# Up projection recomputed from PSUM and two gated products over magnitudes in a quantised feed-forward block

## What is computed

```
def act_qdq(x):                       # 16 bits, one scale for the whole tensor
    scale = jnp.maximum(jnp.max(jnp.abs(x)) / 32767.0, 1e-12)
    return jnp.clip(jnp.round(x / scale), -32768.0, 32767.0) * scale
x    = act_qdq(layernorm(x))
up   = act_qdq(x @ lpbq_dequant(w_up).T)       # 128 -> 384 columns
gate = act_qdq(x @ lpbq_dequant(w_gate).T)
sig  = fixed_qdq_u16(jax.nn.sigmoid(gate))     # 16 bits, fixed scale
gate = act_qdq(gate * sig)
o    = act_qdq(gate * up)
out  = o @ lpbq_dequant(w_down).T
```

## Time and profile before

| | |
|---|---|
| median of 3 runs | 343.34 us (343.32 to 343.42) |
| span of the profiled execution | 341.2 us |
| PE busy | 279.0 us (82%) |
| DVE busy | 252.5 us (74%) |
| ACT busy | 192.6 us (56%) |
| GpSimd busy | 136.7 us (40%) |

### The profile page before, as it was taken

How to read it: one execution, slowest core, us unless ns; L and a number is a source line. 1 busy time by engine, 2 the same in 40 slices (tenths; PEclk the granted TensorE clock), 3 DMA queues, 4 the chain that set the end, 5 groups by cost and what they waited for, 6 DMA issues and landing times. The chain is left out here.

```text
span 341.2 us, 4468 instructions
## 1 busy us (share of the span) xinstructions
PE 279.0 (82%) x1424; PEld 160.7 (47%) x1424; DVE 252.5 (74%) x538; ACT 192.6 (56%) x303; POOL 136.7 (40%) x274
## 2 busy tenths in 40 slices
PE   0889899899989779985007888899998998999994
PEld 0558544455434345331005776664654654444462
DVE  5699875877996388889989977986596693441834
ACT  1673367556476746779589632446656446665232
POOL 6669893750050411870002059921386207131100
PEclk9999999999999999997556999999999999999998
DMA  7930100010000000000000002220001000000004
GB/s 204 336 146 3 69 32 10 27 73 10 1 8 3 0 0 2 1 0 0 1 0 0 2 0 92 94 100 2 10 25 76 8 0 10 1 0 3 0 1 123
DMA packets 9687, 12.55 MB, mean 37 GB/s; under 512 B 896, under 2 KB 5376, under 8 KB 9664
## 3 DMA queue, kind: packets, MB, share of 16 engines
q1 hardware_dynamic: 9232, 11.80, 9.7%
q10 hardware_dynamic: 432, 0.47, 0.7%
HBM read 4.27 MB, written 1.05 MB: 16 GB/s over the span
## 5 line engine op out<-in xcount | busy, mean ns | idle before, releaser
L1333 DVE TENSOR_REDUCE sb_nm<-ps_top 128x3 f32<-128x462 f32 (+2 forms) x168 | 96.0, 626 | 26.6 <-PE ps_top L953 13.9
L772 ACT ACTIVATE sb_pr<-ps_score 128x512 f32<-128x512 f32 (+1 forms) x148 | 82.3, 583 | 58.8 <-PE ps_score L985 49.2
L953 PE MATMUL ps_top<-sb_Kd,sb_Q 128*128 128x462 f32 (+3 forms) x240 | 69.7, 349 | 4.7 <-DVE sb_nm L1333 2.4
L985 PE MATMUL ps_score<-sb_Q,sb_Kd 128*128 128x512 f32 x119 | 54.4, 467 | 1.3 <-ACT sb_pr L772 1.0
L953 PEld LDWEIGHTS ps_top<-sb_Kd,sb_Q 128*128 128x128 f32 x240 | 42.6, 188 | 18.1 <-DVE sb_nm L1333 11.9
L626 POOL TENSOR_SCALAR sb_var<-sb_mv 128x4 f32<-128x4 f32 x16 | 4.7, 291 | 83.3 <-DVE sb_mv L1296 82.9
L985 PEld LDWEIGHTS ps_score<-sb_Q,sb_Kd 128*128 128x128 f32 x119 | 22.2, 188 | 31.6 <-ACT sb_pr L772 23.4
L1017 PE MATMUL ps_pv<-sb_pr,sb_V 128*32 128x512 f32 x256 | 34.1, 605 | 0.0
L620 POOL TENSOR_SCALAR_AFFINE_SELECT sb_pr<-sb_pr 128x512 f32<-128x512 f32 x16 | 10.6, 661 | 46.4 <-ACT sb_pr L772 46.4
L1353 DVE STREAM_TRANSPOSE sb_oq<-ps_pv 128x512 f32<-128x512 f32 x16 | 10.8, 700 | 12.4 <-PE ps_pv L1017 12.3
L643 POOL TENSOR_SCALAR sb_xn<-sb_xr,sb_nmean,sb_rstd 128x128 f32<-128x128 f32 x44 | 19.3, 453 | 1.2
(11 more groups left out here) (180 smaller groups left out, 556.5 us busy)
## 6 DMA issues: line engine op xcount, KB each, us to landing
sb_Q<-sb_qh SPq DMA_DIRECT2D x16, 256.0 KB, 2.3
sb_Q<-sb_ql SPq DMA_DIRECT2D x8, 256.0 KB, 3.3
sb_xr<-x SPq DMA_DIRECT2D x4, 256.0 KB, 7.7
out<-sb_xr SPq DMA_DIRECT2D x4, 256.0 KB, 2.5
sb_wsb<-w SPq DMA_DIRECT2D x1, 704.0 KB, 9.0
sb_wf<-wffn SPq DMA_DIRECT2D x1, 576.0 KB, 8.6
sb_wkr<-wkr SPq DMA_DIRECT2D x2, 256.0 KB, 7.1
sb_Q<-sb_nmT SPq DMA_DIRECT2D x16, 32.0 KB
```

The source lines that it names most:

```text
L772: act.activation(pr[:, k % PRING, q0:T], score_bank(B * layer + b, t)[:, q0:T], ACT.Exp, scale=SCALE).then_inc(exp_r, 1)
L953: ins = pe.matmul(cols[:, c0:c1, :], Q4[n % 3][:, g, P * qt:P * qt + P], Kd[n % 3][:, g, j:j + c1 - c0, 0:keys], start=True, stop=not mask ...
L985: ins = pe.matmul(ps[:, :], Kd[n % 3][:, g, j, 0:P], Q4[n % 3][:, g, :], start=True, stop=True, skip_group_check=True)
L1333: dve.tensor_reduce(nm[:, :, :].rearrange("p t h -> p (t h)")[:, f0:f0 + heads], top[k % MRING][:, 0:keys * heads].rearrange("p (h k) -> p ...
```

## The change

Twelve up tiles are multiplied three times instead of once. Tiles 12 to 23 serve only DVE's maximum, which now reads PSUM. Tiles 24 to 35 are read from PSUM by ACT for the magnitudes, tiles 36 to 47 for the signed 16-bit form. No fp32 copy of up is kept. Gate tiles are reduced by DVE in PSUM first and copied by ACT afterwards. gate16 of batch 1 moves to ACT. For batches 2 and 3 (BY_SIZE) the gated product is taken over magnitudes, in one instruction with its maximum; the sign of the gate is multiplied onto the signed up (`signs`, `signed_up`), and last16 uses these. Batch 0's last16 and last product go in thirds, all on ACT; batch 2's last16 goes in thirds too. down(3) moves behind maximum unit 2 of layer 1 and ffn_residual(3) behind unit 6. q_low moves ahead of statistics 1, and GpSimd's clears move.

On PE:

```diff
+        def up_bank(t):
+            return fbank[t % FRING] if t < 43 else (fbank[1], fbank[2], fbank[3], fbank[6], fbank[0])[t - 43]
...
             def down(c):
-                pe.wait_ge(*((xo_r, c) if c > 0 else (xod_r, 1)))
-                for t in range(TT):
-                    for m in range(NF):
+                for m in range(NF):
+                    if c == 0 or m == 0:
+                        pe.wait_ge(xo_r, m + 1 if c == 0 else NF + c)
+                    for t in range(TT):
...
                             scores_for_top(layer, b, u)
+                            if (layer, i, b, u) == (1, -1, 0, 2):
+                                down(B - 1)
...
+                    def bank_read(t):
+                        if t < 12:
+                            pe.wait_ge(fev, t + 1)
+                        elif t < 24:
+                            pe.wait_ge(fam_r, t + 1)
+                        elif t < 36:
+                            pe.wait_ge(uabs_r, t - 23)
+                        else:
+                            pe.wait_ge(u16_r, t - 35)
...
                         if t >= FRING:
-                            pe.wait_ge(fev, t - FRING + 1)
-                        pe.matmul(fbank[t % FRING][:, :], wfT[:, 3 * (t // 12) + m, :], xq[:, c, :],
+                            bank_read(t - FRING if t < 46 else t - 5)
+                        pe.matmul(up_bank(t)[:, :], wfT[:, 3 * (t >= 12) + m, :], xq[:, c, :],
                                   start=True, stop=True).then_inc(fmm, 1)
...
-                    for k in range(2, 4):
-                        global_top(k)
-                    pe.wait_ge(fev, 24)
-                    pe.wait_ge(o_r, 2)
-                    keep_warm(6)
+                    for t in range(13):
+                        linear(t)
+                    global_top(1)
+                    for t in range(13, 31):
+                        linear(t)
+                    global_top(2)
+                    for t in range(31, 36):
+                        linear(t)
+                    global_top(3)
+                    for t in range(36, 45):
+                        linear(t)
                     global_top(4)
-                    keep_warm(2)
+                    for t in range(45, 48):
+                        linear(t)
                     pe.wait_ge(sc_r, 5)
-                    keep_warm(4)
-                    for c in range(3):
+                    pe.wait_ge(u16_r, 5)
+                    keep_warm(2, score[1])
+                    for c in range(2):
                         down(c)
                     turn_normed("pre", 1, 0)
                     project_q(1, 0)
-                    down(3)
+                    down(2)
                     turn_normed("pre", 1, 1)
+                    pe.wait_ge(u16_r, 12)
```

On ACT, the new queue behind the copies of the gate tiles (`up(c)` is three pieces of 512, each waiting for its tile):

```diff
+                    gate16(1)
                     for c in range(B):
-                        up_size(c)
-                    for c in range(B):
-                        product_size(c)
-                    up16(0)
-                    up16(1)
-                    product16(2)
-                    up16(2)
-                    product16(3)
-                    up16(3)
-                    product(1)
-                    product(2)
-                    product(3)
+                        if c in BY_SIZE:
+                            gate_size(c)
+                        sigmoid16(c)
+                    for t in range(24, 36):
+                        up_size(t)
+                    product_size(0)
+                    product_size(1)
+                    product_size(3)
+                    up(0)
+                    product16(1)
+                    up(1)
+                    for m in range(NF):
+                        product(0, slice(m, m + 1), m + 1)
+                    up(2)
+                    product(1, slice(0, NF), NF + 1)
+                    up(3)
+                    product(2, slice(0, NF), 2 * NF + 1)
                     copy_normed("pre", 1, 0)
                     copy_q(1, 0)
+                    product(3, slice(0, NF), 2 * NF + 2)
```

On DVE, the new instructions and the queue behind the last gate tile (as it stands after the change):

```diff
+                def gated_size(c):
+                    dve.wait_ge(s16_r, c + 1)
+                    dve.wait_ge(gabs_r, c - 1)
+                    dve.tensor_tensor_reduce(out=flat(gf, c), in0=flat(gabs, c - BY_SIZE[0]), in1=flat(s16, c), scale=1.0,
+                                             scalar=0.0, op0=ALU.mult, op1=ALU.max,
+                                             accum_out=amax[:, 3, c:c + 1]).then_inc(am_r, 1)
+
+                def signs(c):
+                    dve.wait_ge(g16_r, c)
+                    dve.tensor_scalar(flat(sign, c - BY_SIZE[0]), flat(g16, c), -1.0, 1.0, ALU.max, ALU.min).then_inc(sign_r, 1)
+
+                def signed_up(c):
+                    dve.wait_ge(sign_r, c - 1)
+                    dve.wait_ge(u16_r, NF * c + NF)
+                    sg = flat(sign, c - BY_SIZE[0])
+                    dve.tensor_tensor(sg, up16(c).rearrange("p m t -> p (m t)"), sg, ALU.mult).then_inc(us_r, 1)
```

On GpSimd:

```diff
             def clear_early():
-                pool.wait_ge(fmm, 24)
-                pool.wait_ge(o_r, B)
+                pool.wait_ge(fmm, 4 * 12)
+                pool.wait_ge(n3_r, NF)
                 pool.memset(Q4[1][:, :, :].bitcast(F32), 0.0).then_inc(q4_clear, 1)
+                pool.memset(Q4[2][:, :, :].bitcast(F32), 0.0).then_inc(q4_clear, 1)
```

More of the change, by code:

```diff
@@ L1184, in _, with linear @@
                     keep_warm(3, top[1])
-                    for t in range(24):
+                    def bank_read(t):
[7 more added lines that the diff above has]
+                            pe.wait_ge(u16_r, t - 35)
+                    def linear(t):
                         c, m = t % 12 // 3, t % 3
@@ L1470, in outer @@
[L1470 to L1476 removed]
+                    dve.wait_ge(uabs_r, NF * c + NF)
@@ new lines, in outer, with last16 @@
+                    dve.wait_ge(*((n2d_r, 1) if c == 2 else (n2abs_r, min(c, 2) + 1)))
+                    dve.tensor_tensor_reduce(out=flat(uabs, c), in0=n2abs(c).rearrange("p m t -> p (m t)"), in1=flat(uabs, c),
+                                             scale=1.0, scalar=0.0, op0=ALU.mult, op1=ALU.max,
+                                             accum_out=amax[:, 4, c:c + 1]).then_inc(o_r, 1)
+                def last16(c, m=slice(0, NF)):
+                    part = lambda t: t[:, m, :].rearrange("p m t -> p (m t)")
+                    if c in BY_SIZE:
+                        dve.wait_ge(us_r, c - 1)
+                        left, right = n2abs(c), sign[:, c - BY_SIZE[0], :, :]
+                    else:
+                        dve.wait_ge(*((n2_r, 1) if c == 0 else (n2a_r, 1)))
+                        dve.wait_ge(u16_r, NF * c + m.stop)
+                        left, right = g16[:, c, :, :], u16[:, c, :, :]
+                    dve.scalar_tensor_tensor(out=part(uabs[:, c, :, :]), in0=part(left), scalar=sc[:, 4, 3:4], in1=part(right),
@@ L1512, in ffn @@
-                for t in range(14, 24):
+                for t in range(19, 24):
                     absmax(t)
                 part_max(2, 12)
-                gated(2)
+                gated_max(1)
                 whole_top(2)
                 scale_of(2)
-                gated_max(2)
-                gated(3)
-                gated_max(3)
+                for c in BY_SIZE:
+                    gated_size(c)
                 part_max(3, B)
+                signs(2)
                 whole_top(3)
@@ L1523, in ffn @@
                 scale_of(3)
-                product16(0)
-                factor(1, 1.0, sc[:, 3, 1:2], sc[:, 2, 1:2])
-                for c in range(B):
-                    outer(c)
-                part_max(4, B)
-                product16(1)
+                product_size(2)
+                factor(1, 1.0, sc[:, 3, 1:2], sc[:, 2, 1:2])
+                outer(2)
+                outer(0)
+                outer(1)
+                outer(3)
+                part_max(4, B)
+                product16(0)
@@ L1530, in ffn @@
                 whole_top(4)
                 scale_of(4)
-                last16(0)
-                dve.wait_ge(n3_r, 1)
-                dve.tensor_scalar(flat(gf, 0), flat(n2abs, 0), sc[:, 4, 1:2], None, ALU.mult).then_inc(xod_r, 1)
+                for m in range(NF):
+                    last16(0, slice(m, m + 1))
                 last16(1)
-                last16(2)
+                signed_up(2)
                 ffn_residual(0)
                 norm_stats("pre", 1, 0)
-                last16(3)
+                for m in range(NF):
+                    last16(2, slice(m, m + 1))
@@ L1540, in ffn @@
+                signs(3)
                 norm("pre", 1, 0)
                 ffn_residual(1)
+                signed_up(3)
+                last16(3)
+                q_low(1, 0)
                 norm_stats("pre", 1, 1)
                 ffn_residual(2)
-                q_low(1, 0)
-                norm("pre", 1, 1)
-                ffn_residual(3)
```

(3 more changed lines are left out.)

123 lines of the change are left out of this document (61 added, 62 removed).

## The result

The changed kernel takes 347.17 us, median of 4 runs (345.93 to 347.55); the kernel before takes 343.37 beside it (343.32 to 343.42). The ratio is 1.0104, 95% interval 1.0086 to 1.0122: slower by 3.8 us. The profiled execution is the fastest of the four, 345.93 with a span of 344.0, against 341.2 before.

A forecast was written before the change was run, and what follows sets the result against it. No engine alone bounds the quantised block, but a chain of global maxima through DVE and PE. With +0.4 at layer 1's start and +3.5 in its ramp, 343.34 + 3.9 = 347.2 us, range 342.2 to 349.8.

The forecast's parts named there:

- Scale 1: Start of the quantised block: DVE reduces gate tiles in PSUM without ACT's copy first; ready at 145.85, gain 0.55.
- Scale 2: Quantised block, batch 2's turn of DVE's queue and PE's spreading: 165.6, gain 2.8, or 4.3 if the clock holds.
- Scales 3 and 4: Later quantised block: scale 3 at 172.2, gain 3.5; scale 4 at 182.4, gain 5.5.
- Half given back before the norm: Scale 4 to batch 0's norm: down(0) waits behind tile 47 until 189.1; norm at 196.4, gain 2.8.
- signed_up: DVE's product of sign and up around batch 0's norm: 1.8 us each, only signed_up(3) on the path.
- The query path: Behind batch 0's norm: takes 3.35 as before; q_low starts at 201.6, ends at 202.35, gain 2.1.
- Layer 1 released by GpSimd: Border to layer 1: PE starts 5.5 behind q_low's end, after batch 1's norm and transpose, at 207.85, 0.4 later.
- down(3) in the ramp: Layer 1's first maximum units: 2.8 for the matmuls plus 0.7 for the residual, 3.5 us added.
- (1): PE's clock holds in every gap: layer 1 starts at 204.75, the ramp adds 3.5, 344.1 us; chance 0.17.
- (2): Scales' gain reaches layer 1, down(3) fits between units: layer 1 at 202 to 203, 338.6 to 341.7 us; chance 0.16.
- (3): Colder: layer 1's first units with down(3) run at 1.2 GHz, 1.7 more, 348.9 us; chance 0.12.
- (4): GpSimd's clearing holds DVE, or GpSimd's root comes late, 1.6 more, 348.8 us; chance 0.05.

The follow-up runs named there:

- after: The changed kernel itself, with nothing further edited; 347.17 us.
- a1_down3_back: Changed kernel with down(3) back ahead of batch 1's transpose and ffn_residual(3) back behind statistics 2; 344.16 us.
- c1: b4 with the gated product over magnitudes and its maximum as two instructions instead of one; 337.88 us.
- b4: a4 plus dummy matmuls ahead of tile 26 and of batch 0's transpose; 336.14 us.
- a3: Changed kernel with up(2) ahead of the thirds of product(0) on ScalarE; 342.52 us.
- b1: Changed kernel with dummy matmuls in four PE gaps, no work moved, one PE wait now ahead of batch 1's transpose; 342.95 us.
- a2: Changed kernel with batch 1's statistics back ahead of q_low on DVE; 344.14 us.
- b3: Kernel before the change with q_low put ahead of statistics 1 on DVE; 346.70 us.
- a4: Changed kernel with the edits of a1_down3_back, a2 and a3 together; 339.39 us.
- b2: Kernel before the change with down(3) put behind maximum unit 2 and ffn_residual(3) behind unit 6; 348.32 us.

## Why the prediction came out right, and where it did not

The forecast of 347.2 stands beside 347.17, but the profiled execution is 345.93, and a closeness of 0.03 is luck: errors that cancel, and a clock that differs from execution to execution. What was right is the mechanism, step by step:

- **Scale 1**, 145.85 by the sum: ready at 145.67, with a gate16 taken up at 145.71. Right.
- **Scale 2**, 165.6 with a fall of the clock, 164.1 without: 163.88 in after's profile, which held, and 165.55 in that of a1_down3_back, where it fell. Both branches were sized to 0.3; which is taken changes from execution to execution, and the sum could name only one.
- **Scales 3 and 4**: 16.8 from scale 2 to scale 4 by the sum, 16.80 in the profile. The fused products, signs under the spreading, the end of the 2.65 beside GpSimd's clearing, all as told; c1 prices the fusing at 1.4 to 1.9, in b4.
- **Half given back before the norm**: tile 47 at 3.2 behind scale 4 by the sum, 3.5 measured; down(0) at 6.7 against 7.0; the norm at 14.0 against 14.5. The mechanism is the one named, and a3 shows it by taking it away: 4.7 us at down(0). One reading in it is wrong: DVE's 2.45 us (last16(2) in thirds and signs) were said to cover GpSimd's root, whose rows come to 1.67 + 1.03 = 2.7 and some 0.1 of handing over. In after the root's last row ends at 195.11, signs at 195.07, and the norm starts at 195.21, 0.10 behind the root as in the kernel before. So the root still releases the norm, at a cost of about 0.2 us.
- **signed_up**, mis-sized: 1.8 taken, 0.96 measured. The nearest row was of another operation. signs took 0.55 where 0.5 was taken. The Trainium skill ("VectorE: DVE Perf Modes", the perf-mode tier table) has tensor_tensor at two elements a cycle where all is 16-bit, and the prediction's estimate from it was 0.9; the trace agrees.
- **The query path**, missed: q projection at half clock, 2.00 where 1.10 stands in b1, so that the path took 4.24 where 3.35 was taken. DVE waited 0.87 for it, which took up the 0.84 that signed_up had saved. q_low came 5.36 behind the norm, 5.2 by the sum.
- **Layer 1 released by GpSimd**: transpose and unit 0 5.2 behind the end of q_low against 5.5. Right in kind; a2 and b3 show it both ways.
- **down(3) in the ramp**, 3.5 by the sum: 2.95 in after, which is DVE's 2.21 of idle time and the residual's 0.74. The 2.8 for the matmuls were partly covered by units 0 to 2. a1 takes it away.
- **Layer 1's first score**, missed: 0.74 later still, with a wait of 0.90 for the DMA of the turned maxima, where there was none before. Why that DMA lands later is open.

So the shifts are -0.96, +2.95 and +0.74, together 2.7 of the 2.8 between the spans, where the sum had +0.4 and +3.5. With the clock lost at tile 26, 1.7 more, it would be 4.4. The median of four, 3.8 above before, lies between. In the case that the forecast assumed, with the fall, the shifts would thus be 4.4 and not 3.9.

**The rivals.** (1) The clock holds everywhere, 344.1: b1 made it so and gave 342.95; 1.2 less than the rival's time, since unit 0 came at 204.10 where 204.75 was forecast, and the ramp cost 2.9 where 3.5 was. (2) The gain reaches layer 1, 338.6 to 341.7: not in the change. a4, where down(0) follows the rounding by 2.3 us, gave 339.39, in the rival's range; but its down(3) was taken out of the ramp and does not fit between the units as the rival had it, and layer 1 started at 203.96, not before 203.3. (3) Colder: not in after's profile, but in a3, b2 and b3, at 1.6 to 1.8 (17.95 and 17.93 against 16.38, 15.27 against 13.43), near the 1.7 of the prediction. (4) GpSimd's clearing: its two clears end at 189.91, before the root for batch 0 is asked for at 192.74; the root itself cost about 0.2, as said above, and not 1.6.

## What to carry to other kernels

Here a chain made 7 us shorter brought nothing, since the queues behind it were in the wrong order for the new pace. After such a cut, follow each in-order queue to the next border and ask, for every step moved, what gap it filled before and who stands behind its new wait. A matmul that fills a gap can pay twice, in its own time hidden and in the clock that the next matmuls have (b2: 4.5 us in the ramp for 2.84 us of matmuls and a residual of 0.74). Where PE waits between short bursts on a path of dependences, try a few dummy matmuls in each gap before anything else, and look at the spread of the runs as well as at their median.

## What the runs showed of the hardware that was not expected

- The same gap of 2.45 us ahead of the same tile left PE at 2.4 GHz in two profiled executions and at 1.2 GHz in three. One more or less of these is 1.5 to 1.7 us, half a per cent of the kernel. The versions with four gaps of 2.5 us and more, or most of them, repeat less well: a1, a2 and a3 spread over 3.6 to 3.7 us in ten runs each, b1 with dummies in the gaps over 1.4 in eleven.
- VectorE on 1536 elements a partition, all int16: 0.55 us for an operation with a constant (signs), 0.96 for a product of two tensors (signed_up), but 1.75 to 1.82 for the product of two tensors with rounding or with a maximum (last16, outer). A plain product of two int16 tensors written as fp32 took 1.76 in c1. So both the form of the instruction and the type of every tensor in it decide.
- GpSimd beside VectorE: in the timeline of GpSimd in after, the root's two instructions for batch 0 stand beside VectorE's thirds of last16(2), those for batch 1 beside other work:

```profile
192.74 0.60 POOL L638 TENSOR_SCALAR sb_var<-sb_mv 128x4 f32<-128x4 f32 x1 [2.82 <-DVE sb_mv L1340]
193.42 1.69 POOL L640 TENSOR_TENSOR sb_rstd<-sb_var,sb_half 128x4 f32<-128x4 f32 x1
...
202.60 0.20 POOL L638 TENSOR_SCALAR sb_var<-sb_mv 128x4 f32<-128x4 f32 x1 [7.49 <-DVE sb_mv L1340]
202.89 1.01 POOL L640 TENSOR_TENSOR sb_rstd<-sb_var,sb_half 128x4 f32<-128x4 f32 x1
```

They take 2.3 and 1.2 us for the same work, as 1.67 and 0.20 stood in the earlier trace rows. That the two engines hold each other up is argued from these rows; no run tried it alone.
